# A first round in another order, a tanh behind the copies of q, and v projected in two pieces

## The reference

```python
def _ada_rmsnorm(x, t, gamma_w, beta_w):
    return (t @ gamma_w.T)[:, None, :] * _rmsnorm(x) + (t @ beta_w.T)[:, None, :]
...
    attn = jax.nn.softmax(scale * jnp.einsum('bnqd,bnkd->bnqk', q, k), axis=-1)   # 16 heads of 16
    o = jnp.einsum('bnqk,bnkd->bnqd', attn, v)
...
    x = x + a_alpha * _attention(_ada_rmsnorm(x, t, attn_gamma_w, attn_beta_w), W_q, W_k, W_v, W_o)
    return x + f_alpha * _swiglu(_ada_rmsnorm(x, t, ffn_gamma_w, ffn_beta_w), gate_w, hidden_w, out_w, out_b)
...
    out = (input - mean) * jax.lax.rsqrt(var + EPS) * weight + bias
    out = out + jnp.tanh(convInfo @ lin_w.T + lin_b)[:, None, :]
    return out * weight + bias
```

## Time and profile before

| | |
|---|---|
| median of 3 runs | 530.4 us (530.06 to 531.44) |
| the profiled execution | 530.51 us |
| its span, first to last instruction | 528.6 us |
| mean granted clock of TensorE | 0.969 of full speed |
| PE busy, share of the span | 483.1 us, 91% |
| DVE, ACT, POOL busy | 74%, 45%, 53% |

### The profile page before, as it was taken

How to read it: one execution, slowest core, us unless ns; L and a number is a source line. 1 busy time by engine, 2 the same in 40 slices (tenths; PEclk the granted TensorE clock), 3 DMA queues, 4 the chain that set the end, 5 groups by cost and what they waited for, 6 DMA issues and landing times.

```text
span 528.6 us, 11662 instructions
## 1 busy us (share of the span) xinstructions
PE 483.1 (91%) x4446; PEld 403.3 (76%) x4446; DVE 392.3 (74%) x772; ACT 239.5 (45%) x347; POOL 277.9 (53%) x182
## 2 busy tenths in 40 slices
PE   7768739999999999999999999999999999999990
PEld 4555627788788897889787987889787988798880
DVE  5846635887878688877888787967888788875636
ACT  3454624333836264443725274534635374513240
POOL 3335455646336843585446841594456834517471
PEclk9979968999999999999999999999999999999996
DMA  8483152220540317030640327030721234220121
GB/s 218 145 202 74 59 140 66 61 62 1 145 136 22 81 28 230 21 93 6 161 117 20 79 73 204 2 97 0 202 75 35 64 91 108 62 61 0 41 57 63
DMA packets 36234, 45.00 MB, mean 85 GB/s; under 512 B 3312, under 2 KB 30704, under 8 KB 36208
## 3 DMA queue, kind: packets, MB, share of 16 engines
q1 hardware_dynamic: 36208, 44.64, 31.9%
HBM read 35.97 MB, written 4.47 MB: 76 GB/s over the span
## 4 chain that ended last, share of the span: by engine, by line
PE 80%; DVE 7%; ACT 4%; DMA 3%; POOL 3%; issue 1%; SPq 1%; ACTq 0%; DVEq 0%; POOLq 0%
PE banks L650 32%; PE banks L667 17%; PE banks L466 7%; PE banks L568 6%; PE banks L600 4%; PE banks L502 4%; PE banks L586 3%; PE banks L591 3%; ACT qpair L843 2%; DVE x2n L1065 2%; PE banks L573 1%; PE banks L621 1%; DMA work_c<-x2n 1%; DMA xtok<-x_in 1%; PE banks L531 1%
## 5 line engine op out<-in xcount | busy, mean ns | idle before, releaser
L650 PE MATMUL banks<-x2s,gh 128*128 128x512 f32 x768 | 193.3, 401 | 8.9 <-ACT x2s L898 8.4
L650 PEld LDWEIGHTS banks<-x2s,gh 128*128 128x128 f32 x768 | 141.3, 190 | 41.6 <-issue 9.0
L1426 POOL TENSOR_TENSOR hs<-act_t,hs 128x512 fp32r<-128x512 f32 x64 | 83.1, 1302 | 99.9 <-ACT hs L879 99.9
L667 PE MATMUL banks<-wout,hs 128*128 128x256 f32 x768 | 104.5, 286 | 1.3 <-POOL hs L1426 1.3
L667 PEld LDWEIGHTS banks<-wout,hs 128*128 128x128 f32 x768 | 97.7, 188 | 6.6 <-POOL hs L1426 1.7
L879 ACT ACTIVATE hs<-act_t 128x512 fp32r<-128x512 f32 x64 | 40.3, 630 | 90.5 <-DVE act_t L1200 84.5
L1196 DVE SCALAR_TENSOR_TENSOR act_t<-act_t,banks 128x512 f32<-128x512 f32 x64 | 43.9, 686 | 49.5 <-ACT act_t L872 49.2
L872 ACT ACTIVATE act_t<-banks 128x512 f32<-128x512 f32 x64 | 38.3, 598 | 84.4 <-PE banks L650 81.6
L1147 DVE RECIPROCAL work_c<-banks 128x512 f32<-128x512 f32 x16 | 53.7, 3354 | 10.3 <-PE banks L586 10.3
L1200 DVE SCALAR_TENSOR_TENSOR act_t<-act_t,banks 128x512 f32<-128x512 f32 x64 | 44.0, 687 | 5.4 <-PE banks L650 1.2
L466 PE MATMUL banks<-xs,wqk 128*128 128x512 f32 x192 | 46.8, 393 | 0.7 <-ACT xs L813 0.7
(11 more groups left out here) (120 smaller groups left out, 699.2 us busy)
## 6 DMA issues: line engine op xcount, KB each, us to landing
xtok<-x_in SPq DMA_DIRECT2D x8, 512.0 KB, 5.4
xres<-x_in SPq DMA_DIRECT2D x8, 512.0 KB, 7.1
row_aa<-rows_dram SPq DMA_DIRECT2D x16, 256.0 KB, 6.8
row_af<-rows_dram SPq DMA_DIRECT2D x16, 256.0 KB, 5.5
row_b<-rows_dram SPq DMA_DIRECT2D x16, 256.0 KB, 6.1
shift<-rows_dram SPq DMA_DIRECT2D x16, 256.0 KB, 6.1
work_c<-xn SPq DMA_DIRECT2D x14, 256.0 KB, 3.8
y<-final SPq DMA_DIRECT2D x7, 512.0 KB, 3.2
```

The lines of the kernel that those rows point to most:

```text
L650: last = mm(banks[:, base + part, :], gh[:, a, k, w:w + P], x2s[:, b, k, :], start=(n == 0), stop=(n == 5))
L667: last = mm(banks[:, t // 2, D * (t % 2):D * (t % 2) + D], hs[:, c % 2, b, P * t:P * t + P], wout[:, a, c, :], start=(c == 0 and a == b an ...
L1426: tt(hs[:, c % 2, 1, :], act_t[:, c % 2, :], hs[:, c % 2, 0, :].bitcast(F32), ALU.subtract)\
```

## The change

Four things are moved; no arithmetic of a steady round is added or removed.

1. **First round.** PE's `o_proj(0)` stands ahead of `k_proj(1)` and `v_proj(1)`; the transposes of x2 stand ahead of `q_proj(1)`. The input of group 1 is no longer loaded transposed and normalised on POOL, but scaled on POOL by token, transposed on PE (8 transposes) and scaled and shifted on DVE. The cuts of the weights stand earlier on ACT and POOL, `sel` is built on ACT, `move_v(0)` is issued ahead of the loads of stages 5 and 6. 16 matmuls that only keep PE busy stand ahead of `o_proj(0)`, 4 ahead of `transpose_x2(0)`; 18 others are gone.
2. **tanh.** `tanh(f, 0)` stands behind all four copies of `pair_q`, not between them; it is now in `main`.
3. **v.** `v_proj(g)` makes tiles 0 to 2 only (`V_EARLY = 3`). Tile 3 is made by `v_rest(g)` in bank 0 behind `scores_for_max(g, 1)`. `keep_v` is two instructions; `place_v_kept(g)` moves behind `tanh(f, 1)`, `place_v_swapped(g)` behind `feed(f, 2)`.
4. **Last low part.** POOL's `hidden_lo(f, 7)` waits until DVE has scaled all of x2 (`x2n_scaled`).

```diff
@@ SP @@
             load_stage(3)
-            store_rs(1)
             load_stage(4)
-            load_rs(1)
+            move_v(0)
             load_stage(5)
             load_stage(6)
-            move_v(0)
...
             def move_v(g):
-                sp.wait_ge(v_out, g + 1)
+                sp.wait_ge(v_out, 2 * g + 1)
@@ PE @@
+            def v_rest(g):
+                if rowed(g):
+                    pe.wait_ge(x3_steps, X3 * (g - 1))
+                project_v(-(V_EARLY // 2), range(V_EARLY, TT))
...
             def ffn_out(f, c):
+                if c == 0 and not is_last(f):
+                    pe.wait_ge(v_out, 2 * (f + 1) + 1)
...
             def main(g):
                 gate_hidden(f, 0)
                 scores_for_max(g, 0)
                 scores_for_max(g, 1)
+                v_rest(g)
                 gate_hidden(f, 1)
@@ ACT @@
             def head(g):
                 k_out(g)
                 keep_v(g)
-                place_v_kept(g)
                 x2_split(g - 1)
-                pair_q(g, (1,))
-                tanh(g - 1, 0)
-                pair_q(g, (0,))
+                pair_q(g)
...
             def main(g, ln=True):
-                hidden_hi(f, 0)
+                feed(f, 0)
+                keep_v(g, rest=True)
+                tanh(f, 1)
+                place_v_kept(g)
+                hidden_hi(f, 1)
+                if not later(f):
+                    cut_hi(8)
+                feed(f, 2)
                 place_v_swapped(g)
-                for c in range(1, 4):
-                    feed(f, c)
-                    if c == 1 and not later(f):
-                        cut_hi(8)
+                feed(f, 3)
                 exp(g, 0)
@@ DVE first() @@
                 normalise(0, 1)
+                for k in range(KD):
+                    scale_shift_xn(1, k, x0_steps, 4 + 2 * k).then_inc(xn_beta if k else x0_steps, 1)
                 residual1(0)
@@ POOL first() @@
-                gamma_xn(1)
-                scale_xn(1)
-                shift_xn(1)
-                xs_split(1)
+                pool.wait_ge(norm1_steps, RS * 2)
+                tt(xtok[:, :, :], xtok[:, :, :], nt1[:, 1, 0, :].unsqueeze(2).to_broadcast([P, TT, D]),
+                   ALU.mult).then_inc(xs_scaled, 1)
+                finish_shift()
                 cut_lo(2)
...
@@ POOL main() @@
                 xs_split(g + 1)
+                pool.wait_ge(x2n_scaled, TT * (g + 1))
                 hidden_lo(f, 7)
```

More of the change, by code:

```diff
@@ L220, in is_last, with rowed @@
             return isinstance(g, int) and g == GROUPS - 1
-        def v_kept(g):
-            return flat(xn if later(g) else x2n)
+        def rowed(g):
+            return not isinstance(g, int) or g > 1
         def bank_of_s(g, n):
@@ L279, in load_x @@
             def load_x(g):
-                if not later(g):
+                if not rowed(g):
+                    if g:
+                        sp.wait_ge(xt_mm, 1)
                     sp.dma_start(xtok[:, :, :], x_v[g]).then_inc(ld_x, 16)
                     return
-                if isinstance(g, int) and g == 1:
-                    sp.wait_ge(xt_mm, 1)
+                if isinstance(g, int):
+                    sp.wait_ge(xt_mm, 2)
                 sp.wait_ge(x_stats, XS * g)
@@ L499, in v_proj, with project_v @@
                     pe.wait_ge(p_ready, 4)
-                for t in range(TT):
+                project_v(base, range(V_EARLY if later(g) else TT))
+            def project_v(base, tiles):
+                for t in tiles:
                     for n, (k, a, b) in enumerate(passes):
@@ L670, in ffn_out, with head @@
                 last.then_inc(out_mm, 1)
[L672 removed]
+            def head(g, ln=True):
                 k_proj(g)
                 v_proj(g)
+                if not ln:
+                    warm_up(wqk[:, 0, 0], WARM_NORM, 0)
                 transpose_x2(g - 1)
[L677 removed]
+                if ln:
+                    ffn_out(g - 2, CH - 1)
                 q_proj(g)
@@ L699, in first @@
                 attend(0, 1)
-                k_proj(1)
-                v_proj(1)
+                transpose_x(1)
+                warm_up(wqk[:, 0, 0], WARM_OUTPUT, 2)
                 o_proj(0)
[L703 to L706, removed]
             def main(g):
@@ L844, in pair_q, with keep_v @@
                                              scale=cst[:, C_PAIR + j:C_PAIR + j + 1]).then_inc(qpair_ready, 1)
-            def keep_v(g):
-                act.wait_ge(v_mm, g + 1)
-                nc.scalar.activation(v_kept(g), banks[:, bank_of_v(g):bank_of_v(g) + 2, :].rearrange("p k n -> p (k n)"),
+            def keep_v(g, rest=False):
+                act.wait_ge(v_mm, 2 * g + 1 if rest or not later(g) else 2 * g)
+                tiles = range(V_EARLY, TT) if rest else range(V_EARLY if later(g) else TT)
+                base = -(V_EARLY // 2) if rest else bank_of_v(g)
+                src = banks[:, base + tiles[0] // 2:base + tiles[-1] // 2 + 1, :].rearrange("p k n -> p (k n)")
+                skip = D * (tiles[0] % 2)
+                nc.scalar.activation(v_kept[:, D * tiles[0]:D * (tiles[-1] + 1)], src[:, skip:skip + D * len(tiles)],
                                      ACT.Copy).then_inc(v_out, 1)
@@ L931, in first @@
                 place_v_kept(0)
-                act.wait_ge(setup_dve, SETUP_TANH)
-                nc.scalar.activation(cvec, cvec, ACT.Tanh).then_inc(setup_act, 1)
+                cut_hi(2)
+                cut_hi(3)
                 place_v_swapped(0)
@@ L985, in last @@
                 f = g - 1
-                hidden_hi(f, 0)
+                feed(f, 0)
+                keep_v(g, rest=True)
+                tanh(f, 1)
+                place_v_kept(g)
+                hidden_hi(f, 1)
+                feed(f, 2)
                 place_v_swapped(g)
-                feed(f, 1)
-                feed(f, 2)
                 exp(g, 0)
```

98 lines of the change are left out of this document (41 added, 57 removed).

## The result

The changed kernel takes **564.5 us** (median of 4 runs, 561.2 to 567.8) against 530.8 us for the kernel before in the same runs: ratio 1.0635, 95% interval 1.0571 to 1.07. The profiled execution took 564.46 us, span 562.6 us, mean granted clock 0.941 against 0.969.

A forecast was written before the change was run, and what follows sets the result against it. PE, holding 80% of the chain that ended last, was taken as the bound. The terms -18.4 + 7.4 + 46.2 - 0.5 = +34.7 us took the 528.6 us span to 563.3; with 1.9 outside, 565 us, range 547 to 579.

The forecast's parts named there:

- the four parts of the sum: Changes forecast for the first round up to its landmark (-18.4 us), round 1 (+7.4), rounds 2 to 6 (+46.2), round 7 (-0.5).
- Part 1, the gap: PE's 1.23 us wait ahead of the second score block goes; a steady round gains about 1.17 us before new costs.
- Part 1, the port: On DVE, one stats_x2 tile falls from 1.49 to 0.41 us behind the moved low part; x2n comes 1.08 us sooner.
- Part 1, the late move_v: On SP, load_x goes behind the later move_v and costs nothing, at most 0.5 us if late.
- Part 2, the stall: The late scatter delays SP's loads, row_b and POOL's low part; PE stalls 8.2 us per round in ffn_out(f, 2).
- The bound: Upper limit on PE's stall per round: not above 9 us, as the queue ahead of load_b is thinner.
- Part 3, the clock: PE's clock falls to half in the stall; slow work behind it costs 2.2 us per stall, bounds 0 and 2.4.
- The rival with the clock up: PE's clock stays up, or the stall is short: 552 us, or 547 with the shortest landing as well; chance 0.20.
- Part 4, the first round: With o_proj(0) starting 9.5 us earlier, round 1's landmark, the start of gate_hidden(0, 0), comes at 60.3 us, 18.4 earlier.
- Round 7: Last round: the scatter holds up nothing, row_b shifts 8 us but is wanted 27 us in; -0.5 us.
- row_b is there in time: Rival: keep_x2 on POOL starts early enough that no round stalls, 503 us; chance 0.10.
- The first round gives back half: Rival: k_proj(1) waits for xs_split(1) and matmuls run at half clock; 9 us lost gives 574 us; chance 0.10.

The follow-up runs named there:

- e10: The changed kernel with load_b(f) issued a round earlier, ahead of move_v(f + 1), for f = 1 to 6; 511.1 us.
- e12: e11 with tanh(f, 0) put back between the copies of q; 510.6 us.
- e14: e11 without POOL's wait for x2n ahead of hidden_lo(f, 7); 503.1 us.
- e5: The kernel before with only place_v_swapped(g) moved behind feed(f, 2), move_v still early and v in one piece; 591.6 us.
- e1: The changed kernel with load_af and load_b issued ahead of load_xt on SP; 549.9 us.
- e3: The changed kernel with 30 useless matmuls between second and third pass of ffn_out(f, 2) in rounds 1 to 6; 554.0 us.
- e9: The kernel before with cut_hi(6) ahead of pair_q(1) on ACT; 525.7 us.
- e11: The changed kernel with load_b ahead of move_v for f = 1 to 6, and keep_x2(0) behind hidden_lo(0, 3) in round 1; 500.8 us.
- e2: The changed kernel with keep_x2(f) behind hidden_lo(f, 3) on POOL; 505.2 us.
- e4: The changed kernel with place_v_swapped(g) one feed earlier, ahead of feed(f, 2); 558.5 us.
- e13: e11 without the 16 useless matmuls ahead of o_proj(0); 500.5 us.

## Why the prediction was right, and where its argument was not

**Total.** 565 forecast, 564.5 measured; each of the four parts of the sum within 1.3 us. That the total is off by only 0.5 is partly luck: the first round came out 1.2 us better and round 7 1.2 us worse than forecast, and single runs of this kernel lie between 561 and 568 us. A steady round adds up from the runs: 57.04 (e10) + 8.30 + 2.4 = 67.7, and 67.64 was measured.

**Part 1, the gap.** Right: 1.23 us forecast, and undoing it costs 9.8 us, 1.3 to 1.5 in each of seven rounds (e12). A round without stalls is 57.04 us, 1.4 shorter than before where 1.17 was forecast.

**Part 1, the port.** The mechanism was right (1.50 against 0.41 us, e14), the size not. "If x2n stays as late, the 0.72 us is waited away" failed: 0.2 us per round is lost without the wait. (The prediction's 0.66 in place of 1.17 us says 0.5; its own 0.72 would say 0.7.)

**Part 1, the late move_v.** This is the weak step of the argument. "`load_x` goes behind the later `move_v` ... nothing, and at most 0.5 us if late" asks only when x is wanted, not what else stands behind `move_v` on SP: every load of the round, `load_b` among them. In rounds 1 to 6 of the changed kernel the price of nothing held, since the scatter is later still: the stall is 8.15 us on average, and 8.1 in e5, where `move_v` is early. By e1 it alone makes `keep_x2` 5.1 us late and keeps most of the stall.

**Part 2, the stall.** The chain (scatter, `load_xt`, `load_b`, `keep_x2`, `hidden_lo(f, 2)`, PE) is right: e5 has it alone, at 591.6 us. In round 3 of the changed kernel `keep_x2` starts 9.82 us behind the end of the scatter, where 9.91 was taken over. 8.2 us were forecast, 8.15 measured. The bound did not hold: "not above 9" was said, and round 2 has 10.08. POOL is idle for 14.6 us on average ahead of `keep_x2` in rounds 2 to 6, not about 12. What was incomplete is that the scatter was taken for the only cause. The two are in series in SP's list and the later one, the scatter, decides, so the total came out right. "It needs `load_b` issued some 8 us earlier than the scatter allows" was incomplete for the same reason: e1 freed it from the scatter and gained 15 us, not 61.

**Part 3, the clock.** Right: the clock falls in the stall, third pass and gate lose 0.5 + 1.9 = 2.4 us against 2.2 forecast, and filling the stall gives 1.8 to 2.0 per stall back (e3). The rival with the clock up is out.

**Part 4, the first round.** Landmark 59.05 against 60.3, and here two terms miss in opposite directions. `o_proj(0)` starts at 44.15 (45 forecast). From the end of `residual1(0)` to the end of x2n it is 5.20 us (49.28 to 54.48), not the 6.93 taken over from before. From there to the landmark it is 4.57, not 3.35; the transposes stand behind 4 matmuls that keep PE busy, and `q_proj(1)` waits 0.27 us for a copy of k. e9 shows the late cut to be worth 4 to 5 us by itself; the rest is argued from the new order.

**Round 7.** -0.5 forecast, +0.7 measured; this is the late `move_v` once more, with no scatter ahead of `load_b`. The failed words are "it is wanted 27 us into the round": before, `keep_x2(6)` starts at 444.91, T + 12.9. Now POOL and PE show:

```profile
486.44 2.40 POOL L1413 TENSOR_TENSOR x2c<-x,row_b 128x1024 f32<-128x1024 f32 x1 [10.74 <-issue]
...
497.44 0.74 PE L673 MATMUL banks<-wout,hs 128*128 128x256 f32 x4 [0.89 <-POOL hs L1437]
```

`keep_x2(6)` starts at T + 21.2, 8.3 us later. POOL is busy from there to the low part that PE then waits 0.89 us for. With `load_b` ahead of `move_v` (e10, e11) this wait is gone and round 7 takes 96.06 us, 0.6 less than before, as forecast.

**Rivals.** "row_b is there in time" gave 503; e11, which brings this about in rounds 2 to 6, runs at 500.8, and e2, where `row_b` is as late but nothing urgent waits behind it, at 505.2. "The first round gives back half" is out by the landmark at 59.05; of its reasons, `k_proj(1)` does wait for `xs_split(1)`, but only 1.59 us.

## What to carry to other kernels

When an item of an in-order queue becomes late, list everything behind it on that queue, not only the load it stands next to; two late items in series hide each other, and freeing one shows the other. Where a step of no urgency waits for a transfer, no urgent step should be queued behind it: moving one POOL instruction past two others was worth 59 us here. A long wait on TensorE costs its own length and then the slow clock behind it, here 8.15 + 2.4 us.

## What was not expected of the hardware

- The time that SP needs to issue a DMA is not fixed. In round 3 the two DMAs of `load_af` took 1.42 us in the changed kernel and 3.76 in e4, the two of `load_b` 1.42 us and 2.12 in e1. Both slow pairs come at the end of a closely packed series of loads, seven or eight issues within 7 us; why they are slow is not shown.
- Rounds in which PE hangs on a DMA's landing vary: rounds 2 to 6 take 66.4 to 69.1 us in one execution of the changed kernel. Those of e10 and e11, in which it does not, are equal to 0.01 us (57.04 and 57.05).
- 24 matmuls that ran slower (4.76 against 3.23 us, e13) cost nothing, since a wait of 1.57 us stood behind them: the clock counts only on the path.
